# Ending a one-core attention and expert kernel's block without GpSimd's drain

## The reference, cut to what matters

```
x = x + xattn(layernorm(x), ctx, ctx, mask, gamma, beta)   # x: 8 x 256 x 256, ctx: 8 x 77 x 256
x = x + ffn(layernorm(x), w_gate, w_gate_up, w_down)

def ffn(x, ...):                      # 8 experts, 2 of them per token, F = 1024
    gate_probs = top 2 of softmax(x @ w_gate), made to sum to 1
    g, u = split(x @ w_gate_up[e])
    expert_out[e] = (silu(g) * u) @ w_down[e]
    return sum over e of gate_probs[e] * expert_out[e]
```

## Time and profile before

| | us |
|---|---|
| median of 3 runs | 454.46 (453.41 to 454.66) |
| profiled execution, its own time | 454.86 |
| its span, first to last instruction | 453.1 |
| TensorE busy in the span | 433.4 (96%) |
| VectorE busy | 306.7 (68%) |
| ScalarE busy | 216.6 (48%) |
| GpSimd busy | 193.4 (43%) |

### The profile page before, as it was taken

How to read it: one execution, slowest core, us unless ns; L and a number is a source line. 1 busy time by engine, 2 the same in 40 slices (tenths; PEclk the granted TensorE clock), 3 DMA queues, 4 the chain that set the end, 5 groups by cost and what they waited for, 6 DMA issues and landing times.

```text
span 453.1 us, 10145 instructions
## 1 busy us (share of the span) xinstructions
PE 433.4 (96%) x2358; PEld 356.5 (79%) x2358; DVE 306.7 (68%) x757; ACT 216.6 (48%) x461; POOL 193.4 (43%) x207
## 2 busy tenths in 40 slices
PE   8998998989999999999999999999999999999990
PEld 4886556768888888888888888888888888888890
DVE  4878747877678668767865658858875588745540
ACT  3786523464555365544634346446543465434330
POOL 6453112156444444445544345544653335434221
PEclk9999789999999999999999999999999999999996
DMA  7686303355254224534541115533551134221121
GB/s 207 204 258 199 134 12 114 111 141 149 45 153 130 60 35 124 168 71 118 128 130 25 24 25 129 142 104 76 158 129 36 25 78 110 37 38 24 13 25 12
DMA packets 28622, 44.17 MB, mean 97 GB/s; under 512 B 2834, under 2 KB 22220, under 8 KB 28588
## 3 DMA queue, kind: packets, MB, share of 16 engines
q1 hardware_dynamic: 20358, 32.96, 23.5%
q0 software_dynamic: 7520, 10.41, 14.2%
q10 hardware_dynamic: 709, 0.32, 0.3%
HBM read 34.04 MB, written 9.65 MB: 96 GB/s over the span
## 4 chain that ended last, share of the span: by engine, by line
PE 88%; DVE 3%; issue 2%; DMA 1%; ACT 1%; POOL 1%; DVEq 1%; ACTq 0%; SPq 0%; POOLq 0%
PE bank L1415 44%; PE bank L1438 15%; PE bank L1440 8%; PE bank L1428 7%; PE bank L1213 3%; PE bank L1399 2%; PE bank L1320 2%; PE bank L1282 1%; PE bank L1259 1%; PE bank L1292 1%; DMA raw<-in_L_ffn_w_gate_up 1%; PE bank L1245 1%; PE bank L1485 1%; DMA vals<-in_ctx 1%; DVE w L401 1%
## 5 line engine op out<-in xcount | busy, mean ns | idle before, releaser
L1415 PE MATMUL bank<-w,tokT_hi 128*128 (+1 forms) x616 | 169.7, 397 | 1.7 <-DVE tokT_lo L877 0.9
L1133 ACT ACTIVATE gated<-bank,row_rstd 128x512 f32<-128x512 f32 x77 | 53.0, 688 | 177.2 <-PE bank L1415 177.2
L1415 PEld LDWEIGHTS bank<-w,tokT_hi 128*128 128x128 f32 x616 | 110.2, 188 | 23.7 <-issue 1.4
L1438 PE MATMUL bank<-w,aT_hi 128*128 (+1 forms) x304 | 116.7, 418 | 0.0
L886 DVE SCALAR_TENSOR_TENSOR act<-bank,row_rstd,gated 128x512 f32<-128x512 f32 x77 | 57.6, 748 | 79.3 <-ACT gated L1133 79.3
L586 POOL DMA_INDIRECT out<-y_sb,out_i x39 | 62.0, 1589 | 83.7 <-DVE y_sb L907 79.9
L1415 PE MATMUL bank<-w,tokT_lo 128*128 (+1 forms) x308 | 95.3, 391 | 0.0
L1440 PE MATMUL bank<-w,aT_lo 128*128 (+1 forms) x304 | 85.4, 281 | 0.0
L573 POOL TENSOR_TENSOR tok<-tok,beta_b 128x256 f32<-128x256 f32 x36 | 26.3, 731 | 103.3 <-DMA tok<-rows_d,gather_i 103.3
L1415 PEld LDWEIGHTS bank<-w,tokT_lo 128*128 128x128 f32 x308 | 57.8, 188 | 12.6
L1438 PEld LDWEIGHTS bank<-w,aT_hi 128*128 128x128 f32 x304 | 57.2, 188 | 10.7 <-issue 0.3
(11 more groups left out here) (188 smaller groups left out, 425.3 us busy)
## 6 DMA issues: line engine op xcount, KB each, us to landing
raw<-in_L_ffn_w_gate_up SPq DMA_DIRECT2D x32, 512.0 KB, 3.8
raw<-in_L_ffn_w_down SPq DMA_DIRECT2D x16, 512.0 KB, 3.8
rows_d<-x_sb SPq DMA_DIRECT2D x8, 265.0 KB, 4.9
x_sb<-in_x SPq DMA_DIRECT2D x8, 256.0 KB, 7.3
out<-x_sb SPq DMA_DIRECT2D x8, 256.0 KB, 5.0
out<-y_sb,out_i POOLq DMA_INDIRECT x39, 3.8
tok<-rows_d,gather_i POOLq DMA_INDIRECT x38, 4.1
cap<-in_mask_BxSxS_ik SPq DMA_DIRECT2D x1, 462.0 KB, 6.2
```

The costliest lines, as they stand in the source:

```text
L1133: act_e.activation(gated[:, h, :], ps_g[h][:, :], ACT.Silu, scale=row_rstd[:, s:s + 1]).then_inc(gated_set, 1)
L1415: ins = pe.matmul(ps[:, :], tokens_[:, s, k, :], w.rearrange("p a g d -> p (a g) d"), start=(k == 0 and tokens_ is tokT_hi and part == 0), ...
L1438: pe.matmul(ps_y[:, :], aT_hi[:, h, c, :], w.rearrange("p a t d -> p (a t d)"), start=(h == 0 and c == 0), stop=False, skip_group_check=True)
```

## The change

The block is opened with a flag that leaves GpSimd's drain out of its end. The engines then meet at the end by semaphores alone. No other line of the kernel is touched.

```
-        block = stack.enter_context(nc.Block())
+        block = stack.enter_context(nc.Block(no_gpsimd_drain=True))
```

## The result

The changed kernel takes 448.26 us (median of 4 runs, 448.01 to 449.33), the kernel before 454.22 us in the same comparison (4 runs). The ratio is 0.9857, with a 95% interval of 0.9828 to 0.9885: 1.4% faster, and inside the forecast's 446.8 to 449.0. The profiled execution itself reads 448.52 us, with a span of 446.6.

What follows compares the result with a forecast made beforehand. TensorE is busy for 433.4 of 453.1 us, but GpSimd's DRAIN alone was taken to hold the end. -6.52 - 0.03 = -6.55 us, from 454.46 to 447.9 us, range 446.8 to 449.0.

Steps and rivals of the forecast that it cites:

- The hole at the end: After the last add: 9.2 us missing from the timeline, in which GpSimd's DRAIN of 6516 ns alone holds the end.
- -6.52 and -0.03: At the block's end: GpSimd's DRAIN goes, -6.52 us; only one step between sequencer instructions is left around it, -0.03 us.
- The hops: Engines' closing meeting by semaphores: stays at 0.2 us, extra cost 0; bounds 0 and +0.3 us if made engine by engine.
- The four other DRAINs: Other engines' closing DRAINs: may go or stay, cost 0, covered by 4.1 us before GpSimd arrives.
- Entries never retired: GpSimd's DMA issues: retiring old entries could add up to 0.08 us each; taken as 0, bounds 0 and +0.25 us.
- 80 ns per entry: GpSimd's closing DRAIN: walks over 79 finished indirect DMA entries, (6516 - 171) / 79 = 80 ns each.
- Rival A: Behind the program: the launch's closing work takes the drain over, time outside the span 8.3 us, 454.4 us; chance 0.10.
- Rivals B and D: At the next opening: B, DRAIN of about 6.5 us, 454.4 us, chance 0.04; D, dearer retiring, 14.2 us, 462.1 us, chance 0.04.
- Rival C: At the block's end: the flag leaves the DRAIN in or its replacement waits as long, 454.5 us; chance 0.02.

## Why the prediction was right

- *The hole at the end.* Right: the 9.2 us that no timeline row covered held one DRAIN of 6.52 us, and with it gone the span is 6.5 us shorter. Putting it back alone, beside the block's new end, returned them.
- *-6.52 and -0.03.* The spans of the two profiled executions differ by 6.5 us, although the last add was issued 0.1 later; the new span of 446.6 is the forecast 446.55. The device times of these executions differ by 6.34 (454.86 - 448.52), since 1.9 in place of 1.8 us lie outside the span. The medians differ by 5.96 (454.22 - 448.26), 0.6 less than the 6.55 of the sum. The runs of either kernel spread over more than 1 us, and the changed kernel's repeat gave 447.12, which is 7.66 under the kernel before in that comparison. The forecast 447.9 lies between the two medians of the changed kernel.
- *The hops.* 0 was right: GpSimd's two semaphore instructions stand at 446.4 and 446.5 and the others' at 446.6, as close as at 452.9, 453.0 and 453.0.
- *The four other DRAINs.* They stay, over by 442.3. The cover of 4 us was enough.
- *Entries never retired.* 0 was right: the adds' issue times are 1538/1590/1638 ns in the changed kernel, against 1539/1591/1639. With 117 DMAs they are 1576/1624/1637 without the drain and 1575/1623/1636 with it, so that a little more per issue goes with the added DMAs and not with the missing drain.

```profile
L586 POOL DMA_INDIRECT out<-y_sb,out_i x39: 1538/1590/1638, 90.3 to 442.5; - x39
```

- *80 ns per entry.* This was inferred from two DRAINs, where a fixed price fitted as well, and the forecast didn't depend on it. That the runs bear it out was in part luck: 2, 4, 36 and 79 entries give 208, 373, 2992 and 6516 ns, on one line of 81.9 ns each. But I had taken the opening DRAIN's 171 ns as the price without entries, where the line leaves 44 ns; GpSimd's own memsets run beside the opening one. And the line ends somewhere between 79 and 93 DMAs: it would have put the DRAIN of 117 DMAs 1.8 and 5.5 times too long.
- *Rival A*, the launch's closing work takes over: outside the span 1.9 us, where it needed 8.3. Over all kernels run, those that close without GpSimd's drain in the block read 1.9 to 2.0 and the others 1.7 to 1.9; if that is a cost of the flag, it is about 0.1 us. The Trainium skill ("VectorE: DVE Perf Modes", section "The DRAIN you can't avoid") puts the runtime's own DRAINs at about 12 ns each; none of the runs shows one behind the program, and if there is one on GpSimd, it doesn't cost 6.5 us within the measured time.
- *Rivals B and D*, the opening takes over: 171 ns at the opening, in the changed kernel, in its repeat and with 117 DMAs left behind. *Rival C*: the DRAIN is gone.

## What to carry to other kernels

Compare the last row of the timeline with the span: here 9.2 us lay between them, and only the view of the line that closes the block showed that 6.5 of them were a drain of GpSimd. This kernel waits for the landing of its adds by itself, and without the drain nothing that was measured got worse, with 79 DMAs or with 117; more than that was not tried. With the drain in the block, 79 finished DMAs stood uncovered at the end, at 0.08 us each. If it has to stay, place drains in GpSimd's idle time well ahead of the end, behind a gather's landing, so that the closing one finds few entries. One put right behind an add in flight waits for its landing: 2.6 and 4.2 us here, which GpSimd's idle time hid.

## What the runs showed that I had not expected

Beyond 79 DMAs the closing drain isn't longer the more of them the program issues: 79 gave 6.5 us, 93 gave 5.8, 99 gave 5.5 and 117 gave 5.3 or 1.7. A kernel with 38 useless indirect DMAs more read 451.54 us in its one run, 3.5 under the median of the kernel before and 1.9 under its fastest. And a drain seems to wait for a compute instruction of GpSimd in front of it as well: it takes 0.8 us over the line's value behind a tensor operation of 0.73 us, with 2, 24, 27 and 43 entries alike. That reading fits all of these drains; a drain with that tensor instruction moved away was not tried.
